# Four-layer network on one core: in the last layer the first score pass ends 20 items, not 10, before its neighbour's second pass, and half of the rank steps follow it

## What is computed

```python
def _L3_attn_ref(x, qkv_w, qkv_b, out_w, out_b):
    q, k, v = ...                                   # 16 heads
    scores = einsum('bhid,bhjd->bhij', q, k) / sqrt(8) + alibi_bias
    out = einsum('bhij,bhjd->bhid', softmax(scores), v)
    return out @ out_w.T + out_b

def _L3_ffn_ref(x, Wg, W1, b1, W2, b2):             # 16 experts, 160 slots each
    probs = softmax(x @ Wg)
    top1_val, top1_idx = probs.max(-1), probs.argmax(-1)
    vals, idx = top_k(where(top1_idx == expert, top1_val, -inf), 160)
    h = gelu(x_flat[idx] @ W1 + b1)
    out = h @ W2 + b2                               # put back in the token's place
```

## Time and profile before

| | |
|---|---|
| time, median of 3 runs | 2161.23 us |
| the runs | 2155.55, 2161.79, 2161.23 us |
| the profiled execution's own time | 2168.38 us |
| its span | 2166.3 us |
| its mean granted clock of TensorE | 0.805 |
| busy in the span | PE 1581.7 us (73%), DVE 1241.6 us (57%), ACT 1064.4 us (49%), POOL 223.0 us (10%) |

### The profile page before, as it was taken

How to read it: one execution, slowest core, us unless ns; L and a number is a source line. 1 busy time by engine, 2 the same in 40 slices (tenths; PEclk the granted TensorE clock), 3 DMA queues, 4 the chain that set the end, 5 groups by cost and what they waited for, 6 DMA issues and landing times.

```text
span 2166.3 us, 24477 instructions
## 1 busy us (share of the span) xinstructions
PE 1581.7 (73%) x8520; PEld 788.8 (36%) x8520; DVE 1241.6 (57%) x2578; ACT 1064.4 (49%) x1590; POOL 223.0 (10%) x210
## 2 busy tenths in 40 slices
PE   5767667657758979789786677767677578786876
PEld 2443444434524544445443222322222322222442
DVE  4986968949856474664754423224222777673522
ACT  3955946928603323132234766666575022332575
POOL 0430422403300000000000000000000000000003
PEclk9987978879869999999998857667566567876899
DMA  6000000000031001010032311203010121021002
GB/s 251 1 1 0 0 1 0 0 0 0 0 93 38 23 2 52 8 46 15 2 94 110 103 30 41 62 20 98 15 51 22 32 72 53 29 56 53 1 2 64
DMA packets 71567, 83.39 MB, mean 38 GB/s; under 512 B 8864, under 2 KB 68256, under 8 KB 70816
## 3 DMA queue, kind: packets, MB, share of 16 engines
q1 hardware_dynamic: 69760, 77.28, 11.9%
q0 software_dynamic: 1696, 4.72, 0.8%
HBM read 50.77 MB, written 31.20 MB: 38 GB/s over the span
## 4 chain that ended last, share of the span: by engine, by line
PE 44%; DVE 25%; ACT 14%; issue 13%; DMA 2%; SPq 1%; POOL 1%; DVEq 0%; ACTq 0%; POOLq 0%
PE ps L1090 8%; PE ps L828 6%; PE ps L816 5%; DVE neg_max L1787 4%; PE ps L815 4%; ACT scratch L1361 3%; DVE mixture_sum L1533 3%; ACT ps L1343 2%; PE ps L1003 2%; PE ps L955 2%; DVE scratch L1639 2%; DVE gated L1507 2%; DVE hidden L1511 2%; DVE scratch L1628 1%; ACT tanh L1242 1%
## 5 line engine op out<-in xcount | busy, mean ns | idle before, releaser
L1361 ACT ACTIVATE scratch<-ps 128x1024 f32<-128x1024 f32 x272 | 274.4, 1021 | 238.4 <-PE ps L1060 63.2
L1787 DVE TENSOR_REDUCE neg_max<-ps 128x2 f32<-128x1024 f32 (+2 forms) x224 | 232.4, 1068 | 111.0 <-PE ps L1003 109.9
L1090 PE MATMUL ps<-scratch,values 128*32 128x512 f32 (+3 forms) x1280 | 190.3, 681 | 11.2 <-ACT scratch L1361 5.7
L1975 POOL TENSOR_TENSOR scratch<-scratch 128x512 f32<-128x512 f32 x128 | 160.3, 1273 | 361.3 <-DVE scratch L1639 361.3
L1242 ACT ACTIVATE tanh<-ps 128x512 f32<-128x512 f32 x88 | 52.6, 597 | 291.8 <-PE ps L816 291.8
L828 PEld LDWEIGHTS ps<-weights_even,hidden 128*128 128x128 f32 (+1 forms) x960 | 148.6, 227 | 96.7 <-issue 53.2
L828 PE MATMUL ps<-weights_even,hidden 128*128 128x128 f32 (+1 forms) x960 | 156.7, 316 | 34.7 <-DVE mixture_sum L1533 34.7
L1343 ACT ACTIVATE ps<-ps 128x512 f32<-128x512 f32 x256 | 150.8, 589 | 58.4 <-PE ps L1049 58.4
L1634 DVE TENSOR_TENSOR_SCAN scratch<-scratch 128x512 f32<-128x512 f32 x128 | 175.8, 1413 | 1.5 <-ACT scratch L1302 1.5
L816 PE MATMUL ps<-xnt_sequence,weights_even 128*128 128x512 f32 x256 | 151.4, 682 | 0.0
L1507 DVE SCALAR_TENSOR_TENSOR gated<-tanh,ps 128x512 f32<-128x512 f32 x88 | 60.4, 686 | 157.4 <-ACT tanh L1242 157.3
(11 more groups left out here) (286 smaller groups left out, 2724.0 us busy)
## 6 DMA issues: line engine op xcount, KB each, us to landing
scratch<-parts_scratch SPq DMA_DIRECT2D x288, 96.0 KB, 2.3
parts_scratch<-weights_even SPq DMA_DIRECT2D x168, 128.0 KB, 2.4
weights_odd<-in_l SPq DMA_DIRECT2D x1, 4224.0 KB, 28.1
weights_even<-in_l SPq DMA_DIRECT2D x1, 4096.0 KB, 17.2
weights_odd<-in_l SPq DMA_DIRECT2D x1, 4096.0 KB, 13.4
parts_scratch<-gated SPq DMA_DIRECT2D x15, 128.0 KB, 2.4
slots_scratch<-gated SPq DMA_DIRECT2D x5, 256.0 KB, 27.4
weights_even<-slots_scratch POOLq DMA_DIRECT2D x1, 1280.0 KB, 10.3
```

The costliest lines, as they stand in the source:

```text
L1090: mm = pe.matmul(ps[32 * i:32 * i + 32, PV, q0:q0 + n], lhs, buf[:, slot, col:col + n], start=first_, stop=True, skip_group_check=True)
L1361: act.activation(dst, src, ACT.Exp).then_inc(q[l, "exp_done"], 1)
L1787: ins = dve.tensor_reduce(dst, ps[:, base:base + 2, col:col + n], AX.X, ALU.max, negate=True)
L1975: pool.tensor_tensor(l0["y"][:, g, :], l0["y"][:, g, :], l0["hc"][:, g, :], ALU.add)\
```

## The change

```diff
@@ -437,13 +437,16 @@
     cuts = [12, 38, RANKS]
     for b in range(1, NB):
         main = stream[begin[b - 1]:begin[b]]
-        cover = len(main) - 10
+        cover = len(main) - 20
         main = spread(main[:cover], a[b]) + [("mx", l, b, 0)] + main[cover:]
         extras = [(18, ("v", l, b, 0))] if b > 1 else [(2, ("v", l, 1, 0))]
         if b + 1 < NB:
             extras += [(34, ("q", l, b + 1, 0)), (40, ("q", l, b + 1, 1))]
             route = ranks(cuts[b - 1], cuts[b])
-            extras += [(3 + 78 * n // len(route), item) for n, item in enumerate(route)]
+            early = len(route) // 2
+            where = cover + len(a[b])
+            extras += [(3 + (where - 3) * n // early, item) for n, item in enumerate(route[:early])]
+            extras += [(where + 2 + 16 * n // (len(route) - early), item) for n, item in enumerate(route[early:])]
         else:
             extras += [(28 + 3 * n, ("xt", l, 0, n)) for n in range(ST // 4)]
             for p in range(5):
```

## The result

On one chip, in turns with the kernel before: the changed kernel has a median of 2171.24 us (7 runs, 2163.15 to 2177.27), the kernel before 2157.43 us (7 runs, 2146.52 to 2162.85). The ratio is 1.0061 with a 95% interval of [1.0033, 1.0089]: slower by 0.6%, some 13 us. The profiled execution took 2177.27 us, with a span of 2175.1 us (before 2166.3) and a mean granted clock of 0.802. It is the slowest of the seven, 6 us above their median; the profiled execution of the kernel before, 2168.38 us, is 11 us above the median of its own seven. So the two profiles compare well with each other, but both show more than a typical execution takes.

A forecast was written before the change was run, and what follows sets the result against it. PE's waits were taken as what can be won or lost. Packing +12.7, second-pass units +0.9 and the load -4.3 summed to +9.3 us on the 2161.23 us median: 2170.5 us, range 2156 to 2181 us.

The forecast's parts named there:

- SP's order, not `mx`: Start of sequence 1's second pass: SP's stack loads hold the maxima, so an earlier `mx` takes nothing off the 7.10 us.
- (1): First-pass units packed closer: waits on DVE's reductions go from 36 to 48, together +12.7 us.
- (2): Second-pass units behind `mx`: their one slot's waits, with rank steps or first-pass units between some, change by +0.9 us.
- (3): Rank steps on DVE, about 0.75 us each: covered by DVE's idle 0.7 us in a cycle, costed at nothing.
- (4): Section 2's end: the last rank step's place delays the 1,280 KB load; wait for maxima 8.4 us, -4.3 us.
- no meeting: Bound for section 2's return of the maxima: it does not meet the 1,280 KB load, -5.7 us.
- (5): Section 3: no rank steps, experts keep their places, nobody waits for sequence 3's maxima; everything from its second pass on unchanged.
- A: Rival: more waits lower TensorE's granted clock, share down 0.05, another +7 us, 2177.7 us; chance 0.14.
- B: Rival: waits on reductions are DVE's queue; rank steps leaving the packed part free 17 us, 2151.8 us; chance 0.12.
- C: Rival, nearly no change: new short places cost half of 0.85 us and the load is avoided, +1.6 us, 2162.8 us; chance 0.20.
- D: Rival: the load still collides with the maxima's return in section 2, +1.3 in place of -4.3, 2176.1 us; chance 0.12.
- E: Rival: a shorter round trip removes 7.1 us at each of two places; a chance in a hundred, counted in B's.

The follow-up runs named there:

- the packing alone: Kernel before with the first pass packed to end 20 items ahead of the end, rank steps at their old list places; 2181.62 us, ratio 1.0081.
- short counts: Kernel before with each rank-step piece on DVE counting in 64 columns instead of up to 512, experts' part of the result left out; 2141.23 us, ratio 0.9930.
- short counts in the changed kernel: Changed kernel with each rank-step piece on DVE counting in 64 columns, experts' part of the result left out; 2169.66 us, ratio 1.0049 to the kernel before.
- the places alone: Kernel before with only the rank steps moved to the change's list places, first pass spread as before; 2143.80 us, ratio 0.9912.
- the load late: Kernel before with POOL's 1,280 KB load held until the maxima of sequence 2 are back; 2157.80 us, ratio 0.9989.
- the wait filled: Kernel before with 18 and 32 extra matmuls ahead of the waits for the maxima of sequences 1 and 2; 2161.98 us, ratio 1.0007.
- both orders: Kernel before with SP sending the maxima ahead of the last six stack loads and rank steps at the change's list places; 2137.17 us, ratio 0.9901.

## Why the prediction was right, point by point

The forecast was 2170.5 us, 0.43% above the median of before. The change measured 0.61% above it, with 0.43% inside the interval. By the trace, +9.3 us stood against +8.8.

**SP's order, not `mx`.** Right, and shown twice. The wait in section 1 is 7.09 us with `mx` 24.5 us ahead of the end, 7.1 with it 11.3 us ahead and 7.2 with 3.7 us. It falls to 1.2 us when SP sends the maxima first.

**(1) and (2), the packing and the second-pass units.** The sum of the two was 12.7 + 0.9 = 13.6 us. The sections grew by 13.7, and with the packing alone by 14.3. The sign and the total were right, but not what they are made of. The waits on reductions grew by 13.2 us, to 43.8, near the 12.7 of the sum; those on exponentials fell by 2.0 us, to 17.2, where the sum had +0.9. With smaller waits PE stands 10.1 us more (10.5 with the packing alone, 9.6 with the maxima first), and 3.6 us are clock, a term that the sum leaves out. That 12.7 + 0.9 meets 13.7 is in part luck.

The 12.7 us are themselves two misses that cancel. I had 36 waits become 48, all at short places, and nothing behind a values step. Counting in the two traces what stands ahead of each waiting first-pass unit gives this: at the places with a short filling the waits grew from 28.5 us only to 34.8, since of the places with a unit and a rank step only 6 of 11 wait now, for 4.1 us in all (before 12 of 17, for 10.1). But behind a values step alone they grew from 1.6 us (5 of 7 places) to 7.8 us (12 of 15). So it was 57 waits at 0.77 us, and "a values step nothing" was wrong. The two places without any filling waited 1.33 us each, as forecast. The covers shrank to 83.9, 83.4 and 77.9 us; I had said some 78, which holds for section 3 alone.

**(3), the rank steps on DVE at nothing.** This step held for the change, but not for the reason given, and that is luck. I had taken DVE's idle 0.7 us in one cycle of the earlier trace rows as cover for all. In the cover of before a rank step in three pieces holds a reduction back by 0.4 us at full clock; short counts win 0.7% there, the rank steps' new places 0.88%, and the load is at most 0.28% of it. In the packed cover short counts win 0.12%, and the rank steps' places the step from 1.0081 to 1.0061, some 4 us, the size of the load's term; both steps are smaller than their intervals. Had the cover stayed at 10 items, the term put at nothing would have been some -13 to -19 us.

**(4), the load.** I had the load issued 3.5 us behind the end of section 2 and the wait at 8.4 us. It was issued 5.2 us behind it, because the first scatter comes 1.3 us ahead of the end, not 2.8, and the wait is 7.45. The "no meeting" end of the bounds, -5.7 us, was nearly met by -5.3 us. The load alone, held back, gives -5.7 us in the trace and 2 us in the median, 6 at most. (The 8.4 us had been 4.66 us and one and a half times 2.44 us, which is 8.3.)

**(5), section 3.** It has grown by 2.9 us in this profile and by 0.5 us in that of the packing alone, with the same list of items; so its own share can't be told closer. Nobody waits for the maxima of sequence 3.

**The rivals.** A, the clock: the three sections went from 0.77, 0.74, 0.81 to 0.70, 0.76, 0.83; it cost 3.6 us of busy time, about half of what A gave it. B, DVE's queue, which had the time fall: excluded by the result, and its 17 us by the run with short counts in the changed kernel; but it is not wrong for the cover of before, where the places alone won 19 us. (Its sum is 12.7 + 0.9 - 17 - 5.7 = -9.1, not -9.4.) C and D: the places cost more than half of 0.85 us, and the load did not collide. E: excluded by 7.09 us.

What the prediction missed is that TensorE's clock sets the level from which one counts. Of the fourteen profiles of the table seven have 251 to 260 us of PE's busy time in the sections: before, the load late, the wait filled, and all four with 20 items. The other seven have 234 to 242. The timed runs bear this out: the mean granted clock of all executions of a kernel is 0.803 to 0.809 for each of the first seven and 0.811 to 0.818 for each of the others. The two parts of the change, alone +17 and -19 us by their ratios, make +13 us together: with 20 items PE stayed in the upper group in all four kernels, whatever the rank steps did. Which pattern of waits holds the clock up I can tell only from the stretches shown; what decides it for a whole section stays open.

## What to carry to other kernels

Before a producer is moved earlier, look at who holds its result: here the maxima lay ready for 12 us behind stack loads in SP's order, and an edit of that order was worth 1.3%, while packing the first pass to move `mx` forward cost 0.8% by itself. With one buffer that two engines take in turns, room between its uses is the scarce thing; spread them over as many items as the round trip allows (four was the best of those run here, once the order was mended). And split a change in time into busy and standing before explaining it: for the same instructions a change of PE's busy time is its clock. And know where the profiled execution lies among the timed ones: a gain in one stretch of one profile can be a luckier execution.

## What the hardware showed that I had not expected

The same PE instructions of the three sections took from 234.3 to 259.7 us, 25 us of 2160, and it goes with the granted clock. Section 3 shows it best. Seven kernels with 10 items have the very same list there (before, rank steps only, maxima first, load late, short counts, wait filled, both orders), and it took 100.4 to 106.5 us at clocks of 0.88 to 0.81. A cut of DVE's counts moved PE's busy time by 20.8 us while PE stood only 2.4 us less. Falls came behind waits as short as 0.67 us, and behind some of 3 us. Filling an idle stretch with matmuls gained nothing in the times. Two edits that each lowered PE's busy time don't add: -27 and -19 us alone, -21 us together, by their ratios. And one kernel alone goes from 2148.5 to 2169.6 us as its mean clock goes from 0.814 to 0.805. Why the clock settles where it does over a whole section was not found.
